# A feed-forward stage of f32 products, rewritten as f16 high and low parts

## The chip, the cores and the metric

The kernel runs on one core of one Trainium2 chip. The metric is the device time of one execution in microseconds. Engines go by the profile's names: PE (TensorE matmul), PEld (its weight loads), DVE (VectorE), ACT (ScalarE), POOL (GpSimd) and SP (SyncE, here the issuer of DMAs).

## The reference, cut to what matters

Two layers work on 8192 tokens (128 sequences of 64) of 128 features: an mLSTM cell with a mixture of experts, then cross attention and a second feed-forward. Only the last step is rewritten. Each of its 8 experts owns 8 fixed positions of every sequence, so 1024 tokens; there is no routing:

```python
# per expert e, on its 1024 tokens; n = layer norm of x
h = silu(n @ w1[e]) * (n @ w3[e])     # 128 -> 352, w1 and w3 f32
x = x + h @ w2[e]                     # 352 -> 128
```

All inputs and the output are f32.

## The kernel before

The kernel runs five stages, each a block of five hand-ordered engine programs that meet through semaphores. An engine runs its own list in order; a wait holds up all that stands behind it on that engine.

- `phase_moe` (first layer's experts): 16 groups with the shared expert, then 39 tiles of 512 sorted tokens. It already works with f16 parts: weights and activations are split into a high and a low f16, and three f16 products (L1119 to L1121, L1132 to L1134) stand for one f32 product. In the tile part DVE makes `hid` (L1302), ACT the high part (L1196), POOL the low part (L1039). SP loads tile j+5 and stores tile j.
- `phase_attention`: 16 groups of 512 tokens, software pipelined. PE order per group is scores, values, the next group's plain products, and so on; ACT exponentiates the scores (`probs`, L1728) and copies values (`v_out`, L1719); DVE takes maxima (`peak_of`, L1791) and divides (`heads_out`, L1815). POOL gathers rows for group g+4 by indirect DMA (L1524). SP stores each finished group in `x3` (L1503) and, at g = 8, loads the f32 weights of the first two experts.
- `phase_ffn`, the last stage: 16 units of 512 tokens (two for each expert). Per unit `turn` (L1991) transposes the normalised tokens, ACT copies them out (L2032), `up` (L1999, L2000) makes three chunks of 128, 128 and 96 hidden features for w1 and w3, ACT applies silu (L2039), DVE multiplies (L2056), `down` (L2008) sums 12 products into `psY`, and DVE adds `x` (L2062). DVE also does the layer norm: statistics (L260, L265) and four subtract-and-scale instructions of 128x128 (L272); POOL only takes the reciprocal root (L284, L286).

PE's order in a unit of the last stage before:

```python
up(p, 0)
up(p, 1)
if p:
    down(p - 1)
if p + 1 < UNITS:
    turn(p + 1)
up(p, 2)
```

All products of this stage are f32; each matmul of the program appears in the trace as two matmul instructions.

Of the kernel before, what the change touches and what calls it, by code (L numbers as in the profile page):

```python
# [910 lines left out]
def phase_moe(nc, sems, a, s, sw, res, front, given, raw, cell):  # L911
# [4 lines left out]
    with ExitStack() as ctx:  # L916
# [522 lines left out]
def phase_attention(nc, sems, a, s, hb, res, ffn, given, raw, sw, cell):  # L1439
# [3 lines left out]
    with ExitStack() as ctx:  # L1443
# [114 lines left out]
        def _(pe):  # L1558
# [129 lines left out]
        def _(act):  # L1688
# [54 lines left out]
            for g in range(LAST):  # L1743
# [21 lines left out]
        def _(v):
# [131 lines left out]
class Ffn:  # L1897

    def __init__(self, nc, ctx, sems, cell, front, raw):
        NC = len(CHUNKS1)  # L1900
        r = self.room = Room(nc, ctx, sems, "ffn")
        self.ident = front.ident
        at = 6 * GROUP
        self.w1 = [*(r.sb(f"w1{w}", [D, FF1]) for w in range(2)), raw[:, at:at + FF1]]
        self.w3 = [*(r.sb(f"w3{w}", [D, FF1]) for w in range(2)), raw[:, at + FF1:at + 2 * FF1]]
        self.w2 = [*(r.sb(f"w2{w}", [P, NC, D]) for w in range(2)),
                   raw[:, at + 2 * FF1:at + 2 * FF1 + NC * D].rearrange("p (c d) -> p c d", c=NC)]
        self.x = [r.sb(f"x{q}", [P, TILES, D]) for q in range(2)]
        self.x += [raw[:, q * GROUP:(q + 1) * GROUP].rearrange("p (t d) -> p t d", t=TILES) for q in range(4, 6)]
        self.xn = cell.xn[1]  # L1910
        self.ln = LayerNorm(r)
        self.w_in, self.x_in = [r.sem(f"w_in{w}") for w in range(3)], [r.sem(f"x_in{q}") for q in range(4)]
        self.xn_done, self.turned, self.xnT_done = r.sem("xn"), r.sem("turned"), r.sem("xnT")
        self.up_done, self.silu_done, self.h_done = r.sem("up"), r.sem("silu"), r.sem("h")
        self.y_done, self.out_done, self.stored = r.sem("y"), r.sem("out"), r.sem2("stored")

    def load(self, sp, s, p):
        for h in range(2):
            sp.dma_start(self.x[p % 4][h * S:(h + 1) * S, :, :], unit_rows(s["x3"], p, h)).then_inc(self.x_in[p % 4], 16)

    def load_weights(self, sp, a, e):
        w = e % 3
        for dst, src in ((self.w1, "f1"), (self.w3, "f3")):
            sp.dma_start(dst[w][:, :], a[src][e]).then_inc(self.w_in[w], 16)
        sp.dma_start(self.w2[w][:, :, :], a["f2"][e]).then_inc(self.w_in[w], 16)
# [278 lines left out]
```

## Time and profile before

| | us |
|---|---|
| timed runs (3) | 1047.19, 1047.42, 1048.82; median 1047.42 |
| profiled execution, span first to last instruction | 1165.9 |
| its own time | recorded as that span alone |
| profiled span less the median | 118.5 |
| last stage in the profile, first transpose to last addition | 1024.69 to 1162.52 = 137.8 |

The profiled execution is 118.5 us longer than the median run. Absolute durations of single instructions are read from it; the share of a whole stage in a timed run is not known.

In the rows, "busy" is the time in which an engine had an instruction under way; PEclk is the granted TensorE clock as a share of 2.4 GHz; "x" counts instructions; a bracket at the end of a row is the engine's idle time before it and the instruction that ended it.

### The profile page before, as it was taken

How to read it: one execution, taken by the hardware profiler on the slowest of the kernel's cores; microseconds unless marked ns; L12 is line 12 of the kernel's file. 1: busy time of each engine (PE TensorE's matmuls, PEld its weight loads, DVE VectorE, ACT ScalarE, POOL GpSimd, SP SyncE). 2: the span in 40 equal slices, each digit the busy share in tenths (PEclk: the TensorE clock that was granted, in tenths of full speed). 3: DMA queues.
4: the chain of work that ended last, by engine and by line, in shares of the span. 5: the costliest groups of instructions: out<-in, count | busy, mean ns of one | idle time of the engine just before them, and what ended most of it. 6: DMA issues, size and time to landing. Idle time of an engine off the chain costs nothing. (4 is left out here: it accounts for less than half of the span.)

```text
span 1165.9 us, 24805 instructions
## 1 busy us (share of the span) xinstructions
PE 969.0 (83%) x9121; PEld 680.7 (58%) x9121; DVE 734.8 (63%) x2271; ACT 535.2 (46%) x848; POOL 505.3 (43%) x566
## 2 busy tenths in 40 slices
PE   6819998667787749999994478888888899989998
PEld 1217776444444426666662267777777778856665
DVE  7676999765566545877774555554555556445553
ACT  2457886432333325666665134453444446332221
POOL 4202675676566652555555773344533531011110
PEclk9869998677879768999998578888888989999999
DMA  8554553321222235333332111101110210024331
GB/s 258 192 148 138 159 165 106 128 89 51 57 61 66 61 89 149 109 124 123 119 119 82 46 33 33 29 28 38 44 31 29 83 49 21 21 65 111 93 93 36
DMA packets 84600, 101.29 MB, mean 87 GB/s; under 512 B 36129, under 2 KB 57313, under 8 KB 83713
## 3 DMA queue, kind: packets, MB, share of 16 engines
q1 hardware_dynamic: 73552, 81.61, 23.5%
q0 software_dynamic: 8192, 16.79, 4.7%
q10 hardware_dynamic: 2736, 1.31, 0.4%
q8 instruction: 73, 1.20, 0.4%
q14 instruction: 47, 0.38, 0.1%
HBM read 64.81 MB, written 30.67 MB: 82 GB/s over the span
## 5 line engine op out<-in xcount | busy, mean ns | idle before, releaser
L1728 ACT ACTIVATE split_table<-attn_psT 128x1024 f32<-128x1024 f32 x64 | 65.5, 1023 | 170.0 <-DMA early_ctxT<-in_ctxT 95.9
L1039 POOL TENSOR_TENSOR moe_h_lo<-moe_hid,moe_h_hi 128x512 f16<-128x512 f32 x78 | 90.3, 1158 | 100.2 <-ACT moe_h_hi L1196 95.4
L1619 PE MATMUL attn_psO<-heads_vheads,split_table 128*64 128x18 f32 x2048 | 87.2, 220 | 30.1 <-issue 30.0
L1302 DVE SCALAR_TENSOR_TENSOR moe_hid<-moe_psU,split_to_hidden,moe_act_g 128x512 f32<-128x512 f32 x110 | 81.0, 748 | 36.5 <-ACT moe_act_g L1190 36.4
L1190 ACT ACTIVATE moe_act_g<-moe_psG,split_unscale 128x512 f32<-128x512 f32 x110 | 75.7, 688 | 59.7 <-PE moe_psU L1121 38.6
L1619 PEld LDWEIGHTS attn_psO<-heads_vheads,split_table 128*64 128x64 f32 x2048 | 78.3, 148 | 41.6 <-issue 39.7
L1791 DVE TENSOR_REDUCE split_table<-attn_psN 128x16 f32<-128x1024 f32 x62 | 75.8, 1222 | 22.4 <-DMA early_ctxT<-in_ctxT 9.6
L1815 DVE RECIPROCAL split_table<-attn_psO 128x16 f32<-128x16 f32 x64 | 16.5, 257 | 112.7 <-PE attn_psO L1619 50.8
L1033 POOL DMA_INDIRECT scratch_xs<-cell_xn,res_row x64 | 63.3, 989 | 42.4 <-DVE res_row L1296 25.2
L1196 ACT ACTIVATE moe_h_hi<-moe_hid 128x512 f16<-128x512 f32 x110 | 68.5, 623 | 24.3 <-DVE moe_hid L1302 23.3
L1033 POOL DMA_INDIRECT scratch_xs<-moe_xn,res_row x64 | 62.6, 978 | 37.2 <-DVE res_row L1296 19.4
L1524 POOL DMA_INDIRECT cell_h<-scratch_ys,res_slot x64 | 62.0, 969 | 19.9 <-issue 19.9
L1524 POOL DMA_INDIRECT cell_y<-scratch_ys,res_slot x64 | 61.8, 966 | 17.7 <-issue 17.4
L284 POOL TENSOR_SCALAR ffn_shifted<-ffn_mv 128x4 f32<-128x4 f32 x16 | 3.6, 228 | 146.7 <-DVE ffn_mv L265 116.5
L1602 PE MATMUL attn_psT<-attn_queries,attn_keys 64*128 64x128 f32 x640 | 64.4, 320 | 1.4 <-issue 1.4
L1602 PEld LDWEIGHTS attn_psT<-attn_queries,attn_keys 64*128 64x128 f32 x640 | 60.2, 213 | 6.9 <-issue 2.0
L284 POOL TENSOR_SCALAR attn_shifted<-attn_mv 128x4 f32<-128x4 f32 x16 | 3.7, 232 | 138.3 <-DVE attn_mv L265 137.5
L1607 PE MATMUL attn_psT<-res_row,attn_sel 64*128 64x128 bf16 x512 | 62.5, 232 | 1.2 <-issue 1.2
L2056 DVE TENSOR_TENSOR ffn_rest_hT<-ffn_rest_act_g,ffn_rest_psU 128x512 f32<-128x512 f32 (+1 forms) x48 | 32.4, 676 | 41.4 <-ACT ffn_rest_act_g L2039 41.4
L1582 PE MATMUL attn_psN<-attn_keys,attn_queries 64*128 64x256 f32 x320 | 53.9, 462 | 4.4 <-DVE split_table L1791 4.4
L1132 PE MATMUL moe_psY<-moe_wt,moe_h_hi 128*128 128x128 f16 x312 | 54.3, 219 | 1.9 <-DVE cell_h L1321 1.9
L2039 ACT ACTIVATE ffn_rest_act_g<-ffn_rest_psG 128x512 f32<-128x512 f32 (+1 forms) x48 | 28.6, 595 | 57.9 <-PE ffn_rest_psU L2000 57.9
(282 smaller groups left out, 2762.9 us busy)
## 6 DMA issues: line engine op xcount, KB each, us to landing
early_ctxT<-in_keys SPq DMA_DIRECT2D x16, 512.0 KB, 3.5
scratch_ys<-cell_h SPq DMA_DIRECT2D x26, 256.0 KB, 2.0
early_ctxT<-in_values SPq DMA_DIRECT2D x8, 544.0 KB, 3.5
mlstm_vals<-in_values SPq DMA_DIRECT2D x8, 544.0 KB, 3.5
res_x<-in_x SPq DMA_DIRECT2D x16, 256.0 KB, 6.2
early_ctxT<-in_ctxT SPq DMA_DIRECT2D x16, 256.0 KB, 6.5
attn_in_ctxT<-attn_in_ctxT SPq DMA_DIRECT2D x64, 64.0 KB
scratch_x<-split_table SPq DMA_DIRECT2D x16, 256.0 KB
```

Source lines behind the costliest of these rows:

```text
L1033: pool.indirect_dma_start(out=s["xs"], out_offset=bass.IndirectOffsetOnAxis(ap=at, axis=0), in_=xn[g % 4][:, t, :], in_offset=None).then_i ...
L1039: pool.tensor_tensor(h_lo[u % 3][c][:, :], hid[u % 2][c][:, :], h_hi[u % 3][c][:, :], ALU.subtract).then_inc(lo_done[c], 1)
L1132: pe.matmul(psY[:, t, :], hi, down_weights(u, 0, c), start=(c == 0), stop=False)
L1190: act.activation(act_g[c][:, :], psG[c][:, :], ACT.Silu, scale=sw.unscale[:, 0:1]).then_inc(silu_done, 1)
L1196: act.activation(h_hi[u % 3][c][:, :], hid[u % 2][c][:, :], ACT.Copy).then_inc(hi_done[c], 1)
L1302: v.scalar_tensor_tensor(out=hid[u % 2][c][:, :], in0=psU[c][:, :], scalar=sw.to_hidden[:, 0:1], in1=act_g[c][:, :], op0=ALU.mult, op1=ALU ...
L1524: pool.indirect_dma_start(out=picks[g % 2][n][:, t, :], out_offset=None, in_=s["ys"], in_offset=bass.IndirectOffsetOnAxis(ap=at, axis=0)). ...
L1602: pe.matmul(psT[:, at:at + P], keys[g % 3][rows, b, 2 * mp:2 * mp + 2, :].rearrange("p m t -> p (m t)"), queries[g % 3][rows, b, :, :].rea ...
L1607: ins = pe.matmul(psT[:, at:at + P], sel[rows, b, mp, :], shift[rows, :], start=False, stop=True)
L1619: ins = pe.matmul(psO[i % 2][b2 * S:(b2 + 1) * S, at * 2 * VW1:(at + 1) * 2 * VW1], probT[i % 2][:, rr, b2, mp, n * S:(n + 1) * S], vheads ...
L1728: act.activation(probT[i % 2][:, :, :, :, :].rearrange("p r b m q -> p (r b m q)"), psT[:, :], ACT.Exp).then_inc(prob_done, 1)
L1791: v.tensor_reduce(peak[:, :, 2 * i:2 * i + 2, :], plain_bank(g, i)[:, :].rearrange("p (r b m t) -> p r b m t", r=HR, b=2, m=HM), AX.X, ALU ...
```

## The change

1. The raw weights `f1`, `f3`, `f2` become one array `f123`, 1088 f32 columns per expert. During the tile part of `phase_moe` SP loads them in 16 pieces (704 or 384 columns) and DVE takes the largest absolute value of each (`largest`). At the head of attention DVE and PE turn these into scale factors (`scale_vector`, `spread_scales`).
2. In attention groups 1 to 10, one expert per group: SP loads an expert's raw weights, ACT writes the high f16 half (`high`), DVE the low half (`low`), SP stores the table of 2176 f16 columns (544 KB) in a scratch `fw` (`keep`).
3. The last stage loads these tables and uses three f16 products for each f32 product; ACT makes the high parts of `x` and `h`, DVE the low part of `x`, POOL the low part of `h`.
4. The layer norm's subtract-and-scale moves from DVE to POOL. PE's order becomes `turn(p+1)`, `up(p)`, `down(p-1)`. There are six token buffers in place of four, and statistics run three units ahead.

```diff
+    def feed(self, sp, a, n, piece):
+        sp.wait_ge(self.piece_read, ONE + n)
+        sp.dma_start(piece[:, 0:last - first], a["f123"][e][:, first:last]).then_inc(self.piece_in, 16)
+    def largest(self, v, n, piece):
+        v.wait_ge(self.piece_in, ONE + 16 * (n + 1))
+        v.tensor_reduce(self.tops[:, n:n + 1], piece[:, 0:last - first], AX.X, ALU.max,
+                        apply_absolute_value=True).then_inc(self.piece_read, 1)
...
+    def load_raw(self, sp, a, e, raw):
+        sp.wait_ge(self.low_done, ONE + e)
+        sp.dma_start(raw[:, :], a["f123"][e]).then_inc(self.raw_in, 16)
+    def high(self, act, e, raw, table):
+        act.wait_ge(self.raw_in, ONE + 16 * (e + 1))
+        act.wait_ge(self.table_out, ONE + 16 * e)
+        for first, last, scale in self.parts():
+            ins = act.activation(table[:, first:last], raw[:, first:last], ACT.Identity, scale=scale)
+        ins.then_inc(self.high_done, 1)
+    def low(self, v, e, raw, table):
+        v.wait_ge(self.high_done, ONE + e + 1)
+        for first, last, scale in self.parts():
+            ins = v.scalar_tensor_tensor(out=table[:, WIDE1 + first:WIDE1 + last], in0=raw[:, first:last], scalar=scale,
+                                         in1=table[:, first:last], op0=ALU.mult, op1=ALU.subtract)
+        ins.then_inc(self.low_done, 1)
+    def keep(self, sp, s, e, table):
+        sp.wait_ge(self.low_done, ONE + e + 1)
+        sp.dma_start(s["fw"][e], table[:, :]).then_inc(self.table_out, 16)
...
@@ phase_moe, SP and DVE
                 store(j)
+                if j % 2 and j // 2 < len(PIECES1):
+                    fw.feed(sp, a, j // 2, piece)
...
+                n = u - GROUPS - 5
+                if n >= 0 and n % 2 == 0 and n // 2 < len(PIECES1):
+                    fw.largest(v, n // 2, piece)
@@ phase_attention, SP, PE, ACT, DVE
+            fw.load_raw(sp, a, 0, ffn.raw)
...
                 store(g)
-                if g == GROUPS // 2:
+                if 1 <= g <= E1:
+                    fw.keep(sp, s, g - 1, ffn.table)
+                if 1 <= g < E1:
+                    fw.load_raw(sp, a, g, ffn.raw)
+                if g == E1 + 1:
+                    sp.wait_ge(fw.table_out, ONE + 16 * E1)
                     for e in range(2):
-                        ffn.load_weights(sp, a, e)
+                        ffn.load_weights(sp, s, e)
...
+            fw.spread_scales(pe, psO[0])
...
                 if two:
                     v_out(g + 2)
+                if 1 <= g <= E1:
+                    fw.high(act, g - 1, ffn.raw, ffn.table)
...
             hb.clear(v, blank)
+            fw.scale_vector(v, psO[0])
             combine(0)
...
                 if now:
                     heads_out(g, 0)
+                if 2 <= g < E1 + 2:
+                    fw.low(v, g - 2, ffn.raw, ffn.table)
@@ phase_ffn, POOL, PE, ACT, DVE
-            for p in range(1, UNITS):
-                ln.root(pool, p, p % 2)
+            def low_part(p, c):
+                pool.wait_ge(hi_done, ONE + NC * p + c + 1)
+                pool.tensor_tensor(h_lo[p % 2][c][0:m, :], hid[c][0:m, :], h_hi[p % 2][c][0:m, :], ALU.subtract).then_inc(lo_done, 1)
+            ln.root(pool, 1, 1)
+            early.normalise(pool, 1)
+            for p in range(UNITS):
+                if p + 2 < UNITS:
+                    ln.root(pool, p + 2, p % 2)
+                    early.normalise(pool, p + 2)
+                if p:
+                    low_part(p - 1, 2)
+                low_part(p, 0)
+                low_part(p, 1)
...
-                pe.matmul(psG[c][0:m, :], w1[w][:, f:f + m], xnT[p % 2][:, :], start=True, stop=True)
-                pe.matmul(psU[c][0:m, :], w3[w][:, f:f + m], xnT[p % 2][:, :], start=True, stop=True).then_inc(up_done, 1)
+                for w, ps in enumerate((psG, psU)):
+                    pe.matmul(ps[c][0:m, :], early.up_weights(e, w, 0, f, m), x_hi[p % 2][:, :], start=True, stop=False)
+                    pe.matmul(ps[c][0:m, :], early.up_weights(e, w, 0, f, m), x_lo[p % 2][:, :], start=False, stop=False)
+                    ins = pe.matmul(ps[c][0:m, :], early.up_weights(e, w, 1, f, m), x_hi[p % 2][:, :], start=False, stop=True)
...
-                pe.wait_ge(h_done, ONE + NC * (p + 1))
+                pe.wait_ge(lo_done, ONE + NC * (p + 1))
...
             for p in range(UNITS):
+                if p + 1 < UNITS:
+                    turn(p + 1)
+                for c in range(NC):
+                    up(p, c)
                 if p:
                     down(p - 1)
...
                 gate(p, 0)
+                if p:
+                    high_part(p - 1, 2)
                 gate(p, 1)
+                high_part(p, 0)
                 gate(p, 2)
+                high_part(p, 1)
...
             for p in range(UNITS):
+                if p + 1 < UNITS:
+                    low_x(p + 1)
+                if p >= 2:
+                    out_(p - 2)
                 gated(p, 0)
-                if p + 1 < UNITS:
-                    early.normalise(v, p + 1)
                 gated(p, 1)
+                if p + 3 < UNITS:
+                    early.statistics(v, p + 3)
                 gated(p, 2)
```

## Rows read from the trace of the kernel before

**Rows 1.** Windows: stretch, length; PE, PEld, DVE, ACT, POOL busy (count), PEclk, DMA share, GB/s.

```profile
455.00:627.00 172.00, 167.65 (x1539) 112.51 (x1537) 136.82 (x197) 115.10 (x193) 90.25 (x78) 1.00 0.36 114
...
690.00:1024.00 334.00, 296.76 (x4223) 253.22 (x4219) 178.91 (x506) 151.63 (x197) 123.43 (x133) 0.88 0.13 37
1024.00:1163.00 139.00, 134.88 (x640) 85.49 (x640) 74.00 (x236) 39.41 (x65) 18.97 (x30) 0.99 0.30 81
```

**Rows 2.** Chain that ended last, within the last stage: start, duration, what.

```profile
1103.45 2.68 PE ffn_rest_psY L2008 x24
...
1111.72 2.68 PE ffn_rest_psY L2008 x24
```

**Rows 3.** Timeline of PE in one expert tile of the first layer.

```profile
574.75 0.38 PE L1119 MATMUL moe_psG<-moe_x_hi,moe_wt 128*128 128x512 f16 x1
...
576.04 0.22 PE L1132 MATMUL moe_psY<-moe_wt,moe_h_hi 128*128 128x128 f16 x1
...
577.38 0.61 PE L1064 MATMUL moe_psT<-split_ident,cell_xn 128*128 128x128 f32 x4
...
577.83 0.38 PE L1119 MATMUL moe_psG<-moe_x_hi,moe_wt 128*128 128x512 f16 x1
```

**Rows 4.** Instruction groups of POOL, by shape: count, busy us, mean ns, idle before.

```profile
L1039 POOL TENSOR_TENSOR moe_h_lo<-moe_hid,moe_h_hi 128x512 f16<-128x512 f32 x78 | 90.3, 1158 | 100.2 <-ACT moe_h_hi L1196 95.4
...
L286 POOL TENSOR_TENSOR ffn_rstd<-ffn_shifted,ffn_power 128x4 f32<-128x4 f32 x16 | 16.6, 1036 | 1.3
...
L284 POOL TENSOR_SCALAR ffn_shifted<-ffn_mv 128x4 f32<-128x4 f32 x16 | 3.6, 228 | 146.7 <-DVE ffn_mv L265 116.5 <-POOLq L1443 30.2
...
L1043 POOL MEMSET cell_h<- 128x512 f32 x1 | 0.5, 524 | 0.0
...
L866 POOL TENSOR_SCALAR cell_next_shifted<-res_mv 128x16 f32<-128x16 f32 x1 | 0.3, 268 | 0.1
```

**Rows 5.** Instruction groups of DVE, by shape.

```profile
L1302 DVE SCALAR_TENSOR_TENSOR moe_hid<-moe_psU,split_to_hidden,moe_act_g 128x512 f32<-128x512 f32 x110 | 81.0, 748 | 36.5 <-ACT moe_act_g L1190 36.4
...
L272 DVE TENSOR_SCALAR cell_xn<-ffn_x,ffn_mv,ffn_rstd 128x128 f32<-128x128 f32 x32 | 8.9, 345 | 6.4 <-POOL ffn_rstd L286 6.4
...
L172 DVE TENSOR_REDUCE split_tops<-split_w_raw 128x1 f32<-128x2304 f32 x3 | 7.4, 2511 | 0.0
```

**Rows 6.** Instruction groups of ACT, by shape.

```profile
L1190 ACT ACTIVATE moe_act_g<-moe_psG,split_unscale 128x512 f32<-128x512 f32 x110 | 75.7, 688 | 59.7 <-PE moe_psU L1121 38.6 <-issue 12.2 <-remote 5.2
L1196 ACT ACTIVATE moe_h_hi<-moe_hid 128x512 f16<-128x512 f32 x110 | 68.5, 623 | 24.3 <-DVE moe_hid L1302 23.3 <-issue 0.9
```

**Rows 7.** Timeline: the last stage's first transposes and products, and its last addition.

```profile
1024.69 0.63 PE L1991 MATMUL ffn_rest_psT<-split_ident,cell_xn 128*128 128x128 f32 x4 [1.71 <-PEq L1443]
1026.10 1.28 PE L1999 MATMUL ffn_rest_psG<-raw_keys,ffn_w 128*128 128x512 f32 x2 [0.78 <-ACT raw_keys L2032]
...
1161.83 0.69 DVE L2062 TENSOR_TENSOR raw_keys<-ffn_rest_psY,raw_keys 128x512 f32<-128x512 f32 x1 [3.04 <-PE ffn_rest_psY L2008]
```

**Rows 8.** Timeline of one attention group: DVE, SP, ACT and PE.

```profile
788.83 0.26 DVE L1815 RECIPROCAL split_table<-attn_psO 128x16 f32<-128x16 f32 x1 [2.08 <-DMA early_ctxT<-in_ctxT]
...
791.06 24.30 SPq L1503 DMA_DIRECT2D scratch_x<-split_table  x2
...
793.69 1.34 ACT L1719 ACTIVATE heads_vheads<-attn_in_ctxT 64x512 f32<-64x512 f32 x2
799.00 1.02 ACT L1728 ACTIVATE split_table<-attn_psT 128x1024 f32<-128x1024 f32 x1 [3.98 <-DMA early_ctxT<-in_ctxT]
...
802.95 0.63 PE L1602 MATMUL attn_psT<-attn_queries,attn_keys 64*128 64x128 f32 x4
```

**Rows 9.** DMA issues: count, KB each, median us from issue to landing.

```profile
scratch_ys<-cell_h SPq DMA_DIRECT2D x26, 256.0 KB, 2.0
early_ctxT<-in_values SPq DMA_DIRECT2D x8, 544.0 KB, 3.5
```

**Rows 10.** Timeline of DVE at the head of attention.

```profile
641.10 1.14 DVE L1770 SCALAR_TENSOR_TENSOR res_x<-cell_h,res_cw,res_x 128x128 f32<-128x128 f32 x4 [6.14 <-DMA cell_h<-scratch_ys,res_slot]
```

More of the change, by code:

```diff
@@ L908, in __init__, with phase_moe @@
         self.mv = ctx.enter_context(nc.sbuf_tensor("res_mv", [P, GROUPS * TILES, 2], F32))
-def phase_moe(nc, sems, a, s, sw, res, front, given, raw, cell):
+def phase_moe(nc, sems, a, s, sw, res, front, given, raw, cell, fw):
     T4 = TILES * E0
@@ L986, in _ @@
             given.room.start_at_one(sp)
+            fw.room.start_at_one(sp)
             given.load(sp)
@@ L1897, with __init__ @@
 class Ffn:
-    def __init__(self, nc, ctx, sems, cell, front, raw):
+    SLOTS = 6
+    def __init__(self, nc, ctx, sems, cell, front, raw, given):
         NC = len(CHUNKS1)
@@ L1902, in __init__ @@
         self.ident = front.ident
+        self.raw, self.table = r.sb("raw", [P, WIDE1]), r.sb("table", [P, 2 * WIDE1], F16)
         at = 6 * GROUP
[L1904 to L1907, printed above, removed]
+        self.tables = [self.raw[:, :].bitcast(F16), self.table[:, :], raw[:, at:at + WIDE1].bitcast(F16)]
@@ L1917, in load, with down_weights @@
+    def down_weights(self, e, part, c, m):
+        at = part * WIDE1 + UP1 + c * D
+        return self.tables[e % 3][0:m, at:at + D]
     def load(self, sp, s, p):
+        q = p % self.SLOTS
         for h in range(2):
[L1919 to L1925, printed above, removed]
@@ L2031, in xnT_out @@
                     act.wait_ge(up_done, ONE + NC * (p - 1))
-                act.activation(xnT[p % 2][:, :], psT[:, :], ACT.Copy).then_inc(xnT_done, 1)
+                act.activation(x_hi[p % 2][:, :], psT[:, :], ACT.Copy, scale=X_SCALE).then_inc(x_hi_done, 1)
             def gate(p, c):
@@ L2038, in gate, with high_part, low_x @@
                     act.wait_ge(h_done, ONE + NC * (p - 1) + c + 1)
[L2039 to L2041 removed]
+                act.activation(act_g[c][0:m, :], psG[c][0:m, :], ACT.Silu, scale=fw.unscale[0:m, 0:1]).then_inc(silu_done, 1)
+            def high_part(p, c):
+                m = CHUNKS1[c][1]
+                act.wait_ge(h_done, ONE + NC * p + c + 1)
+                if p >= 2:
+                    act.wait_ge(y_done, ONE + p - 1)
+                act.activation(h_hi[p % 2][c][0:m, :], hid[c][0:m, :], ACT.Copy).then_inc(hi_done, 1)
+            xT_out(0)
             for p in range(UNITS):
+                if p + 1 < UNITS:
+                    xT_out(p + 1)
                 gate(p, 0)
+                if p:
+                    high_part(p - 1, 2)
                 gate(p, 1)
[L2045 to L2046 removed]
+                high_part(p, 0)
                 gate(p, 2)
+                high_part(p, 1)
+            high_part(UNITS - 1, 2)
         @block.vector
         def _(v):
+            def low_x(p):
+                v.wait_ge(x_hi_done, ONE + p + 1)
+                v.scalar_tensor_tensor(out=x_lo[p % 2][:, :], in0=psT[:, :], scalar=X_SCALE, in1=x_hi[p % 2][:, :],
+                                       op0=ALU.mult, op1=ALU.subtract).then_inc(x_lo_done, 1)
             def gated(p, c):
```

166 lines of the change are left out of this document (115 added, 51 removed).

## The prediction

> **What bounds the kernel now.** I read the busy time by stage first. In the last stage PE is busy 134.88 of 139 us at a granted clock of 0.99, POOL only 18.97; in the expert tiles, which already use f16 parts, PE is full too, at 1.00; in attention PE is busy 296.76 of 334 us at 0.88 [rows 1]. The chain that ended last shows PE alone in the last stage: two successive `down` begin 8.26 us apart, as they do all along the stage, and PE has no gap in that time [rows 2]. So a unit costs 8.27 us of PE, and 16 units with head and tail run from the first transpose to the last addition, 1024.69 to 1162.52, 137.8 us [rows 7]. Nothing in it runs below full clock but the head. The span of the profiled execution, 1165.9 us, is 118.5 us above the median of the runs; I take the difference that I forecast as the same number of microseconds in both, because the stage that changes most is at full clock and without stalls in the profile, so it has little room to be shorter in a run.
>
> **PE's part of the change.** An expert tile shows what f16 thirds cost. Six `up` matmuls of 512 columns start at 574.75 and the next kind starts at 576.04: 1.29 us, 0.215 each. The 24 `down` matmuls of 128 columns take 576.04 to 577.38, 0.056 each. Four transposes take 577.38 to 577.83, 0.45 us [rows 3]. The new unit has 3 chunks x 2 weights x 3 = 18 `up`, 4 x 3 x 3 = 36 `down` and the same transposes: 18 x 0.215 + 36 x 0.056 + 0.45 = 6.3 us. If PE stayed the bound, a unit would fall from 8.27 to 6.3, and 16 units by 31 us. That is the best end.
>
> **POOL's part.** This is the term that I think decides. POOL now runs, per unit, one small add (0.228), the root (1.036), four subtract-and-scale instructions of 128x128 and three low parts of 1.158 [rows 4]; for the 96-row chunk I take the full price, as 512 columns are walked all the same. Without the four: 0.23 + 1.04 + 3.47 = 4.74 us, and about 0.08 us between instructions (the idle in front of the 16 roots is 1.3 us in all [rows 4]), eight times, 0.6. The trace has no tensor-scalar of 128 columns on POOL. Bounds: a memset of 512 columns takes 0.524, about 1 ns a column at most, so 0.228 + 124 x 0.85 = 0.33 is the low end (0.85 ns: 0.524 less a 0.1 start); the small tensor-scalar grows from 0.228 at 4 columns to 0.268 at 16, 3.3 ns a column, so 0.60 to 0.64 is the high end; two sources cost 1.158 for 512 columns, 2.3 ns [rows 4]. With one source, between memset and two sources, I take 1.5 ns: 0.41 us, nearest to the low end because the 12 columns behind the high end are short and strided. Four make 1.64. POOL's unit: 4.74 + 0.6 + 1.64 = 7.0 us, more than PE's 6.3. In its list POOL must finish root, normalise and the third low part of unit p-1 before it can begin the first low part of unit p, and PE's `down` waits for that third low part; with POOL never idle, PE waits about 0.7 us a unit. DVE (five passes of 0.75, 3.75 us [rows 5], and the statistics that it already makes) and ACT (three silu of 0.688, three high parts of 0.623 and one copy out of PSUM, priced as a silu, 4.6 us [rows 6]) stay under 6.3.
>
> I chained the four engines' lists with these prices from the first transpose. `up` of unit 0 can now begin only when POOL has normalised unit 1, since `turn(1)` stands ahead of it: about 3.9 instead of 1.4 us after the first transpose [rows 7]; the first `down` ends at 17.9 instead of 15.2. Then twelve units at 7.0, the last three (no more norms) at 6.6, 6.2 and 3.9, and the addition: 17.9 + 84 + 16.7 + 0.8 = 119.4 against 137.8, **18.4 us less**. For unit 0 the clock may still be at half, as the first product's 1.28 us shows [rows 7]; I give back 1.0.
>
> **What the edits ahead of the stage cost.** In the expert tiles, 16 pieces: DVE's maximum of 704 columns is at most 2.511 x 704 / 2304 = 0.77 us [rows 5], every second tile. DVE is busy 136.82 of 172 us [rows 1], PE needs the low x it makes one tile later, and the pieces are asked for two tiles ahead. SP's wait for the piece just read delays a tile load by about 1.6 us, against loads five tiles ahead. I price it at nothing; without that cover it is 8 x (0.77 + 0.42) = 9.5 us. At the head of attention DVE stands idle 6.14 us for the first gather [rows 10]; the new chain is eight small operations and two round trips to PE and hides there unless they average over 0.6 us each.
>
> In attention each of 8 groups gets, on ACT, two passes over 1088 columns, 0.623 x 1088 / 512 = 1.32 us [rows 6], and on DVE 0.748 x 1088 / 512 = 1.59 us [rows 5]. DVE's sits ahead of an idle of 2.08 us [rows 8], so it hides. ACT's follows `v_out`, which ends at 795.03; the next exponential starts at 799.00 after 3.98 us idle [rows 8]. But ACT also waits for the raw weights, whose load SP issues behind the group's store at 791.06 and the 544 KB table store. A 256 KB transfer lands in 2.0 us and one of 544 KB in 3.5 [rows 9]: all three together between 3.5 (side by side) and 9.0 (one after another), by the slope of the two rows 7.7. Then ACT runs its 1.32 us from 798.8, and the exponential comes at 800.1, 1.1 us late; PE wants it at 802.95 [rows 8], when it would have been done at 801.1. So it hides too, barely. I charge 0.2 us to each of 8 groups, 1.5 us; the bounds are 0 and 8 x (1.32 + 1.59) = 23 us.
>
> **Sum:** -18.4 + 1.0 + 1.5 = -16 us: 1150 in the profile, 1047.4 - 16 = **1031 us**.
>
> **Rivals.** (a) **POOL is as quick as DVE at one source.** The same instruction takes 0.345 us on DVE [rows 5]. Then POOL needs 6.7 a unit, the two engines alternate, and the stage ends at 116 instead of 119.4: 1028 us. The Trainium skill, GPSIMD Engine Reference, section Engine selection, says just this, one-input work on GpSimd at roughly line rate; no row here shows it. For it: memset's slope. Against: two operations with two pointers per instruction. (b) **POOL is slow at it**, 0.6 us, the slope of the small form. A unit is 7.75 us, the stage 130: 1042 us. (c) **Slower: the splitting lands on attention's path.** Place: ACT's wait for the raw weights, ahead of the next group's first exponential. The 3.98 us idle there may exist only in the profiled execution, which is 118.5 us longer; in a run with tighter groups the load comes late and PE waits for both passes. It decides from 2.2 us a group (17.5 / 8); at its full 23 us the result is 1031 + 21 = 1052 us. For it: the load stands behind two stores. Against: PE itself shows 37 us less than full in that stage, and DVE and ACT are under 55% there [rows 1]. (d) **Almost no change:** waits of about 0.7 us a unit let the clock fall and give back what POOL leaves, so the stage runs at about 8.2 us a unit: 1046 us. Against: the clock stays at 0.99 to 1.00 where PE is at 97% [rows 1]; I expect 90%.
>
> **Chances.** Forecast 0.50, (a) 0.22, (b) 0.12, (c) 0.10, (d) 0.06. The range: low end (a) without the costs ahead of the stage and with the lowest POOL price, 1023; high end (b) with 3 us more in attention, 1045. A change under 0.2%, 2 us, can't be told from none (the three runs spread over 1.6 us). Faster: forecast, (a), (b), and a little of (c), 0.86; the same: (d), 0.05; slower: 0.09. PE at two thirds of its f32 cost is seen in the trace; what is not seen is POOL's price, and that moves the time by 10 us, seldom its sign.
>
> **What would show it.** Right: `down` 7.0 us apart in the last stage, POOL busy over 90% there with the normalise at 0.41 us, PE waiting before `down` for the low part. Wrong: PE without gaps (a), normalise at 0.6 (b), ACT's `high` idle on a DMA and longer groups in attention (c), a clock under 0.9 in the last stage (d). Groups 1 to 10 of attention as long as the later ones would prove the splitting hidden.

## The result, and the profile after

The change made the kernel slower: 1065.86 us (median of 4 runs, 1063.45 to 1074.26) against 1047.31 (4 runs, 1046.39 to 1048.82), a ratio of 1.0182 [1.0142, 1.0222]. The profiled execution of after spans 1061.6 us.

The profile of before that the prediction was read from was an odd execution, 118.5 us longer than the timed runs. So before was profiled again (run b0_again: 1049.57 us, span 1047.8), and the differences below are against that second profile.

> The kernel before, once more, for a second profile. If the profiled execution of 1165.9 us was an odd one, this one spans about 1047 us, attention groups far from its head are about 16.8 us long with PE busy throughout (as the groups without splitting are in the changed kernel), and a unit of the last stage is 8.27 us. If the profile itself slows this kernel, it spans about 1166 us again.

The excess of the first profile lies where the prediction read its idle times. Its attention, from its first instruction to the first transpose of the last stage, takes 395.6 us against 321.5 in b0_again, 74 of the 118.5 us; 44 lie ahead of attention and none in the last stage (137.8 against 138.2). One attention group, from `v_out` to `v_out`, in the first profile and in the second (columns as in [rows 1]):

```profile
769.83:793.69 23.86, 20.70 (x277) 17.61 (x277) 12.69 (x36) 10.65 (x16) 10.40 (x12) 0.86 0.12 34
...
754.53:771.34 16.81, 16.81 (x283) 14.50 (x279) 12.88 (x36) 10.66 (x15) 10.36 (x12) 1.00 0.19 49
```

In an ordinary execution PE is busy in the whole group, so whatever holds PE up there costs time.

Windows of that second profile of before, attention and last stage (columns as in [rows 1]):

```profile
584.68:906.18 321.50, 284.85 (x4402) 241.79 (x4403) 214.56 (x612) 172.37 (x225) 166.76 (x181) 0.92 0.17 47
906.18:1044.40 138.22, 134.88 (x640) 85.43 (x640) 73.99 (x236) 39.45 (x65) 18.93 (x30) 0.99 0.31 82
```

The same windows of after:

```profile
582.62:921.78 339.16, 292.58 (x4409) 244.83 (x4409) 234.42 (x637) 180.56 (x241) 167.51 (x181) 0.91 0.24 71
921.78:1058.15 136.37, 109.79 (x928) 71.87 (x928) 73.82 (x192) 68.62 (x113) 119.88 (x138) 0.95 0.32 83
```

Attention starts 2.06 us earlier and lasts 17.7 us longer; the last stage, which was to give 18.4 us, gives 1.8. Together -2.1 + 17.7 - 1.8 = 13.8 us, the difference of the two spans.

**The last stage.** PE's busy time fell from 134.88 to 109.79 us, POOL's rose from 18.93 to 119.88. POOL's groups there in after, by shape (columns as in [rows 4]; the first three answer to rows of that group):

```profile
L2107 POOL TENSOR_TENSOR ffn_rest_h_lo<-ffn_rest_hid,ffn_rest_h_hi 128x512 f16<-128x512 f32 x32 | 36.6, 1159 | 0.9
...
L369 POOL TENSOR_TENSOR ffn_rstd<-ffn_shifted,ffn_power 128x4 f32<-128x4 f32 x15 | 15.6, 1042 | 1.2
...
L367 POOL TENSOR_SCALAR ffn_shifted<-ffn_mv 128x4 f32<-128x4 f32 x15 | 3.5, 232 | 32.1 <-POOLq L1533 30.4 <-DVE ffn_mv L348 1.7
...
L355 POOL TENSOR_SCALAR cell_xn<-ffn_x,ffn_mv,ffn_rstd 128x128 f32<-128x128 f32 x20 | 15.7, 800 | 0.9 <-POOL ffn_rstd L369 0.9
```

The old items have the old prices. The new one, subtract-and-scale, takes 0.80 us. POOL's timeline shows a whole unit with no gap over 0.2 us:

```profile
952.78 0.23 POOL L367 TENSOR_SCALAR ffn_shifted<-ffn_mv 128x4 f32<-128x4 f32 x1
953.10 1.04 POOL L369 TENSOR_TENSOR ffn_rstd<-ffn_shifted,ffn_power 128x4 f32<-128x4 f32 x1
954.32 3.14 POOL L355 TENSOR_SCALAR cell_xn<-attn_in_ctxT,ffn_mv,ffn_rstd 128x128 f32<-128x128 f32 x4 [0.18 <-POOL ffn_rstd L369]
957.43 3.38 POOL L2107 TENSOR_TENSOR ffn_rest_h_lo<-ffn_rest_hid,ffn_rest_h_hi 96x512 f16<-96x512 f32 x3
960.79 0.23 POOL L367 TENSOR_SCALAR ffn_shifted<-ffn_mv 128x4 f32<-128x4 f32 x1
```

From 952.78 to 960.79 is 8.01 us, a unit; [rows 2] had 8.26. The granted clock is 1.00 in these units (950 to 960, and again 1010 to 1041). The 0.95 of the whole stage comes from its head: 0.51 in the first 8.2 us, and 0.50 to 0.51 from 941 to 947, behind a wait of PE for POOL's low part ahead of the first `down`:

```profile
940.96 0.29 PE L2149 MATMUL ffn_rest_psY<-ffn_raw,ffn_rest_h_hi 128*128 128x128 f16 x1 [3.53 <-POOL ffn_rest_h_lo L2107]
...
940.94:945.00 4.06, 4.04 (x38) 4.05 (x39) 0.75 (x1) 0.00 (x0) 3.44 (x4) 0.50 0.00 0
```

This first `down` takes 4.0 us and ends 23.2 us after the stage's first transpose; the later ones take 2.2.

**Attention.** What the engines waited for in after (total, times, longest), from 640 to 930:

```profile
ACT ffn_table L289 <- DMA ffn_raw<-in_f: 22.3, 7, 4.0
```

L289 is the pass that writes the high half; it runs in groups 1 to 8, the low half's in groups 2 to 9. The timeline of ACT and SP in three groups of after:

```profile
681.97 1.33 ACT L1816 ACTIVATE heads_vheads<-attn_in_ctxT 64x512 f32<-64x512 f32 x2
687.29 1.39 ACT L289 ACTIVATE ffn_table<-ffn_raw,ffnw_all 128x704 f16<-128x704 f32 x2 [3.98 <-DMA ffn_raw<-in_f]
688.58 1.00 ACT L1825 ACTIVATE split_table<-attn_psT 128x1024 f32<-128x1024 f32 x1
...
702.14 0.37 SPq L1594 DMA_DIRECT2D scratch_x<-split_table  x1
702.55 0.59 SPq L301 DMA_DIRECT2D scratch_fw<-ffn_table  x1
703.18 0.45 SPq L283 DMA_DIRECT2D ffn_raw<-in_f  x1
...
708.57 1.39 ACT L289 ACTIVATE ffn_table<-ffn_raw,ffnw_all 128x704 f16<-128x704 f32 x2 [2.55 <-DMA ffn_raw<-in_f]
```

SP issues the raw load (L283) only behind the group's store (L1594) and the store of the last table (L301), and ACT stands 2.55 us for it. While it stands, the exponential behind it (L1825) stands too. In the second profile of before, ACT's timeline has this at the same place:

```profile
754.53 1.34 ACT L1719 ACTIVATE heads_vheads<-attn_in_ctxT 64x512 f32<-64x512 f32 x2
757.16 1.03 ACT L1728 ACTIVATE split_table<-attn_psT 128x1024 f32<-128x1024 f32 x1 [1.28 <-PE attn_psT L1607]
```

So the idle time that was to hide all this is 1.28 us, not the 3.98 of [rows 8]. Windows of after: the last group without a split, and the first three with one:

```profile
660.77:677.58 16.81, 16.81 (x277) 14.50 (x276) 13.85 (x36) 11.81 (x17) 9.59 (x11) 1.00 0.18 49
677.58:700.29 22.71, 20.30 (x277) 16.56 (x276) 16.14 (x41) 11.92 (x17) 12.02 (x13) 0.85 0.28 85
700.29:718.42 18.13, 17.08 (x277) 14.46 (x276) 13.32 (x36) 11.60 (x17) 8.85 (x11) 1.00 0.35 107
718.42:740.99 22.57, 20.36 (x277) 16.67 (x276) 16.14 (x41) 11.81 (x17) 12.14 (x13) 0.85 0.28 87
```

A wait of 2.55 us makes 16.81 into 18.13. The groups with waits of 3.98 and 3.79 us take 22.71 and 22.57: there the granted clock is 0.85. Two shorter windows inside the last of them: first PE stands still for 2.21 of 5 us, then the clock is at the lower of its two levels:

```profile
727.00:732.00 5.00, 2.79 (x37) 2.26 (x37) 4.30 (x12) 4.07 (x6) 2.77 (x3) 0.99 0.20 59
732.00:737.00 5.00, 5.00 (x40) 3.38 (x42) 2.08 (x6) 3.50 (x6) 0.00 (x0) 0.50 0.00 0
```

The eight groups with a split, by the starts of DVE's last addition (678.71 to 833.88), take 155.2 us, 20.7 over eight of 16.81. In the other six the clock is 1.00 and they take 17.4 to 19.2 us. (The head of attention, from its first instruction to the first of these additions, is 3.2 us shorter in this profile than in b0_again; it is 82.0 us in e5 and 79.5 in e2, so it differs between executions.)

### The profile page after: what moved, and what is told of

It is laid out like the page before. It is cut to its first block and busy times, and to the rows that moved or that the text cites. A ratio compares the mean times of both kernels' runs of the same rounds, so it can differ in the third digit from the quotient of the medians.

```text
span 1061.6 us, 25704 instructions
## 1 busy us (share of the span) xinstructions
PE 881.4 (83%) x9415; PEld 626.8 (59%) x9415; DVE 766.2 (72%) x2268; ACT 572.0 (54%) x912; POOL 608.0 (57%) x674
## 5 line engine op out<-in xcount | busy, mean ns | idle before, releaser
L1825 ACT ACTIVATE split_table<-attn_psT 128x1024 f32<-128x1024 f32 x64 | 65.3, 1020 | 92.1 <-PE attn_psT L1703 86.3
L1620 POOL DMA_INDIRECT cell_h<-scratch_ys,res_slot x64 | 62.5, 976 | 19.2 <-issue 19.2
L1715 PE MATMUL attn_psO<-heads_vheads,split_table 128*64 128x18 f32 x2048 | 72.9, 214 | 0.1
L1620 POOL DMA_INDIRECT cell_y<-scratch_ys,res_slot x64 | 62.6, 979 | 17.7 <-issue 17.4
L1715 PEld LDWEIGHTS attn_psO<-heads_vheads,split_table 128*64 128x64 f32 x2048 | 66.5, 140 | 9.0 <-issue 7.8
L1698 PE MATMUL attn_psT<-attn_queries,attn_keys 64*128 64x128 f32 x640 | 56.2, 294 | 4.8 <-ACT split_table L1825 4.8
L2107 POOL TENSOR_TENSOR ffn_rest_h_lo<-ffn_rest_hid,ffn_rest_h_hi 128x512 f16<-128x512 f32 (+1 forms) x48 | 54.5, 1158 | 6.2 <-ACT ffn_rest_h_hi L2187 5.3
L1698 PEld LDWEIGHTS attn_psT<-attn_queries,attn_keys 64*128 64x128 f32 x640 | 52.8, 188 | 8.8 <-issue 6.3
L1219 PE MATMUL moe_psY<-moe_wt,moe_h_hi 128*128 128x128 f16 x312 | 54.3, 219 | 1.9 <-DVE cell_h L1408 1.9
L800 ACT ACTIVATE mlstm_decay<-mlstm_psA 128x512 f32<-128x512 f32 x64 | 37.8, 591 | 32.9 <-PE mlstm_psA L750 32.9
L1220 PE MATMUL moe_psY<-moe_wt,moe_h_hi 128*128 128x128 f16 x312 | 54.3, 219 | 0.0
L1221 PE MATMUL moe_psY<-moe_wt,moe_h_lo 128*128 128x128 f16 x312 | 54.3, 219 | 0.0
L1678 PE MATMUL attn_psN<-attn_keys,attn_queries 64*128 64x256 f32 x320 | 48.1, 421 | 5.5 <-DVE split_table L1892 5.4
L826 DVE SCALAR_TENSOR_TENSOR mlstm_cT<-mlstm_psS,mlstm_decay 128x512 f32<-128x512 f32 x64 | 43.4, 677 | 11.7 <-PE mlstm_psS L755 11.1
```

The costliest lines, as they stand in the source:

```text
L1620: pool.indirect_dma_start(out=picks[g % 2][n][:, t, :], out_offset=None, in_=s["ys"], in_offset=bass.IndirectOffsetOnAxis(ap=at, axis=0)). ...
L1678: ins = pe.matmul(bank[:, rr * 512 + b2 * HM * S:rr * 512 + (b2 + 1) * HM * S], queries[g % 3][rows, b, :, :].rearrange("p n t -> p (n t)" ...
L1698: pe.matmul(psT[:, at:at + P], keys[g % 3][rows, b, 2 * mp:2 * mp + 2, :].rearrange("p m t -> p (m t)"), queries[g % 3][rows, b, :, :].rea ...
L1715: ins = pe.matmul(psO[i % 2][b2 * S:(b2 + 1) * S, at * 2 * VW1:(at + 1) * 2 * VW1], probT[i % 2][:, rr, b2, mp, n * S:(n + 1) * S], vheads ...
L1825: act.activation(probT[i % 2][:, :, :, :, :].rearrange("p r b m q -> p (r b m q)"), psT[:, :], ACT.Exp).then_inc(prob_done, 1)
L2107: pool.tensor_tensor(h_lo[p % 2][c][0:m, :], hid[c][0:m, :], h_hi[p % 2][c][0:m, :], ALU.subtract).then_inc(lo_done, 1)
```

## The experiments

Two theories stood. **P:** POOL's price of subtract-and-scale sets the last stage. **A:** the late raw load sets the attention groups. Rivals: in the last stage PE or the lower clock, in attention the work of the two splitting passes itself.

**e1, subtract-and-scale back on DVE.**

```diff
-            early.normalise(pool, 1)
...
-                    early.normalise(pool, p + 2)
...
+            early.normalise(v, 1)
...
                 gated(p, 0)
+                if p + 2 < UNITS:
+                    early.normalise(v, p + 2)
                 gated(p, 1)
```

> The changed kernel with subtract-and-scale of the last stage back on DVE (between the first two chunks of a unit); POOL keeps the root and the low parts. Theory: POOL's four instructions of 0.80 us hold the last stage at 8.0 us a unit; without them POOL needs about 5 us and a unit falls to 6.5 to 6.7, the stage from about 136 to 112 to 115, the time by 20 to 24 us, to about 1043. Rival: the low parts' chain through ACT and POOL or the single token buffer holds the unit; then it stays at 8.0 and the time at 1066.

Measured: 1042.06 us, ratio 0.994 [0.9923, 0.9958], 24 us under after; units of 6.70 us, the last stage 115.3 instead of 136.4. P holds. But PE's own 6.3 us was not reached. The chain that ended last runs through DVE alone:

```profile
953.27 2.31 DVE cell_xn L355 x4
...
959.98 2.31 DVE cell_xn L355 x4
```

Four that took 0.345 each [rows 5] take 2.31 together. The instructions of this line, ns min/median/max:

```profile
L355 DVE TENSOR_SCALAR cell_xn<-raw_keys,ffn_mv,ffn_rstd x24: 333/340/2217, 926.4 to 1015.6; 128x128 f32<-128x128 f32 x24
```

The median is the old price; single instructions take up to 2.2 us, this longest one beside two of POOL's low parts in a row. e9 and e10 take this up.

**e2, the table's store and the raw load ahead of the group's store.**

```diff
             for g in range(GROUPS):
-                store(g)
                 if 1 <= g <= E1:
                     fw.keep(sp, s, g - 1, ffn.table)
                 if 1 <= g < E1:
                     fw.load_raw(sp, a, g, ffn.raw)
+                store(g)
```

> The changed kernel with SP issuing the table store and the next raw load ahead of the group's own store, which it waits for 4 us later. Theory: ACT stands idle for the raw weights (22 us in 7 waits) because the load is issued late; issued about 4 us earlier it has landed when ACT comes, groups 2 to 9 fall from 18 to 22.7 us to about 17 to 17.5, and the time falls by 14 to 19 us, to about 1049. Rival A: ACT's and DVE's own passes (1.4 and 1.5 us a group) are the cost: groups stay at 18 or more and the time falls by less than 6 us. Rival B: the extra transfers slow the gathers: the same.

Measured: 1049.89 us (6 runs), ratio 1.0023 [1.0002, 1.0045], 16 us under after. Units stay at 8.0. The timeline of SP and ACT shows the load now 3.6 us ahead of the store, and ACT's pass straight behind the copy of values:

```profile
711.09 0.43 SPq L283 DMA_DIRECT2D ffn_raw<-in_f  x1
714.70 0.37 SPq L1594 DMA_DIRECT2D scratch_x<-split_table  x1
...
717.24 1.33 ACT L1816 ACTIVATE heads_vheads<-attn_in_ctxT 64x512 f32<-64x512 f32 x2
718.60 1.39 ACT L289 ACTIVATE ffn_table<-ffn_raw,ffnw_all 128x704 f16<-128x704 f32 x2
```

Groups take 17.43 us: A holds, for 15.8 of the 20.7 us. (ACT's pass also waits for the table's store, which e2 moves too; the profile puts the wait down to the raw load.) The other 0.62 a group is at DVE and POOL:

```profile
718.04 2.68 DVE L355 TENSOR_SCALAR cell_xn<-res_x,attn_mv,attn_rstd 128x128 f32<-128x128 f32 x4
...
718.58 1.28 POOL L1625 TENSOR_TENSOR res_x<-res_x,attn_in_bp 128x512 f32<-128x512 f32 x1
```

DVE's low pass stands ahead of the statistics, POOL's list starts later by about that pass, and its 1.28 us addition falls on DVE's four instructions, which take 1.30 us in b0_again; e7 tests this.

**e3, one expert's split only**; every unit reads the table of expert 0.

```diff
-                if 1 <= g <= E1:
-                    fw.keep(sp, s, g - 1, ffn.table)
-                if 1 <= g < E1:
-                    fw.load_raw(sp, a, g, ffn.raw)
+                if g == 1:
+                    fw.keep(sp, s, 0, ffn.table)
...
-                    fw.high(act, g - 1, ffn.raw, ffn.table)
+                if g == 1:
...
+                    fw.high(act, 0, ffn.raw, ffn.table)
...
-                if 2 <= g < E1 + 2:
-                    fw.low(v, g - 2, ffn.raw, ffn.table)
+                if g == 2:
+                    fw.low(v, 0, ffn.raw, ffn.table)
...
-        sp.dma_start(self.tables[e % 3], s["fw"][e])
+        sp.dma_start(self.tables[e % 3], s["fw"][0])
```

> The changed kernel with only expert 0 split; seven of the eight splits, their raw loads and table stores are left out, and all units of the last stage load expert 0's table. It prices all of the splitting in attention. Theory: seven eighths of about 21 us, so about 1047 us, with groups of 16.8 us from the third on; and 2 to 4 us below the reordered kernel, which keeps the passes. Rival: the attention stage is longer for another reason (scales, the room taken); then it stays near 1066.

Measured: 1047.37 us (10 runs), ratio 0.9986 [0.997, 1.0003]; groups take 16.81 from the third on, units 8.0. What attention lost is lost by the splits and not by the changed code around them; alone, this does not tell the load from the passes; e2 and e7 do.

**e5, e1 and e2 together.**

> Both mends in one kernel: the subtract-and-scale back on DVE and SP's table store and raw load ahead of the group's store. Theory: the two costs are separate (one in attention, one in the last stage) and add up: 16 us and 24 us off the changed kernel, 1066 - 40 = about 1026 us, 0.98 of the kernel before, attention groups 17.4 us and units 6.7 us. Rival: they share something (the room on DVE, the transfers); then it stays at 1032 or more.

Measured: 1031.52 us, ratio 0.9804 [0.978, 0.9827]; groups 17.43, units 6.70, so each part gives in its stage what it gave alone. The total is 5 us above 1065.9 - 16 - 24 = 1026, at the edge of the rival's 1032. In the profile these 5 us lie outside both parts: attention starts 2.5 us later than in e1 and e2 (585.4 against 582.9), and its head is 2.6 us longer, as it differs between executions.

**e6, POOL's price by form.** Units take turns: the old form, two constants, one operation with a pointer, one with a constant, and one instruction of 512 columns; four in five units are not normalised.

```diff
+        if form == 1:
+            for t in range(TILES):
+                ins = eng.tensor_scalar(xn[:, t, :], x[:, t, :], 0.5, 0.125, ALU.subtract, ALU.mult)
+        if form == 2:
+            for t in range(TILES):
+                ins = eng.tensor_scalar(xn[:, t, :], x[:, t, :], self.ln.rstd[p % 2][:, t:t + 1], None, ALU.mult)
+        if form == 3:
+            for t in range(TILES):
+                ins = eng.tensor_scalar(xn[:, t, :], x[:, t, :], 0.125, None, ALU.mult)
+        if form == 4:
+            ins = eng.tensor_scalar(xn[:, :, :], x[:, :, :], 0.5, 0.125, ALU.subtract, ALU.mult)
```

> The changed kernel with four of five units' subtract-and-scale on POOL in another form, so leaving out the proper norm there: two constants in place of two per-token pointers; one pointer and one operation; one constant and one operation; one instruction of 512 columns with two constants. It measures POOL's price. Theory A: the two pointers make it slow: with constants 0.33 to 0.45 us, one pointer about 0.5 to 0.6. Theory B: POOL pays per column whatever the form: 0.75 to 0.80 us in each 128-column form, and 512 columns about 0.23 + 508 x 4.6 ns = 2.5 us.

Measured: 1059.07 us (one run). POOL's groups by shape, in that order:

```profile
L355 POOL TENSOR_SCALAR cell_xn<-attn_in_ctxT,ffn_mv,ffn_rstd 128x128 f32<-128x128 f32 x8 | 6.3, 797 | 0.4 <-POOL ffn_rstd L369 0.4
L2058 POOL TENSOR_SCALAR cell_xn<-ffn_x 128x128 f32<-128x128 f32 x8 | 5.0, 648 | 0.7 <-PE ffn_rest_psT L2144 0.5 <-POOL ffn_rstd L369 0.2
L2061 POOL TENSOR_SCALAR cell_xn<-ffn_x,ffn_rstd 128x128 f32<-128x128 f32 x8 | 4.7, 607 | 0.4 <-POOL ffn_rstd L369 0.4
L2064 POOL TENSOR_SCALAR cell_xn<-raw_keys 128x128 f32<-128x128 f32 x8 | 4.1, 533 | 0.3 <-POOL ffn_rstd L369 0.3
L2066 POOL TENSOR_SCALAR cell_xn<-raw_keys 128x512 f32<-128x512 f32 x2 | 3.9, 1940 | 0.3 <-POOL ffn_rstd L369 0.3
```

A second operation costs 0.115 us (648 less 533), a pointer 0.075 (607 less 533, and half of 797 less 648). With two constants 384 more columns cost 1.29 us, 3.4 ns each. The small instruction of [rows 4] is one operation with one constant, the cheapest of these forms: from its 0.228 us at 4 columns to 0.533 at 128 it grows by 2.5 ns a column, less than the 3.3 that it shows from 4 to 16. Neither theory holds: the forms differ, so it is not a price by column alone, and even with constants none is below 0.53.

**e7, e5 with DVE's low pass behind the statistics.**

```diff
-                if 2 <= g < E1 + 2:
-                    fw.low(v, g - 2, ffn.raw, ffn.table)
                 if three:
                     statistics(g + 3)
+                if 2 <= g < E1 + 2:
+                    fw.low(v, g - 2, ffn.raw, ffn.table)
```

> Both mends, and DVE's low pass of the weights put behind the group's statistics in place of ahead of them. The reordered kernel's groups are still 17.43 us against 16.81: its trace shows DVE's subtract-and-scale in attention at 2.68 us for four in place of 1.30, under POOL's bias add, which the later statistics have moved onto it. Theory: with the statistics at their old place POOL's list keeps its time, the two don't meet, and groups fall to 16.8 to 17.0 us; time 3 to 5 us under the kernel with both mends alone, about 1022. Rival: the two passes' own time is the cost; then groups stay at 17.4.

Measured: 1027.8 us, ratio 0.9784 [0.9768, 0.98]. The window of the eight groups has PE without a gap at full clock, 16.81 each:

```profile
684.30:818.79 134.49, 134.49 (x2202) 116.00 (x2203) 115.90 (x304) 93.34 (x126) 89.32 (x90) 1.00 0.35 108
```

So the splitting hides completely once two lists have another order; the last 0.62 us a group came from the place of DVE's pass. The time is 3.7 us under e5, as expected; the 1022 came from e5's expected 1026.

**e8, e7 with ACT's third high part ahead of the next unit's first silu.**

```diff
-                gate(p, 0)
                 if p:
                     high_part(p - 1, 2)
+                gate(p, 0)
                 gate(p, 1)
```

> The last one, and on ACT the high part of a unit's third chunk ahead of the next unit's first silu in place of behind it. Theory: a unit of 6.7 us still waits in front of its last products for the low part of the third chunk, which follows that high part; earlier it leaves PE's own 6.3 us plus what DVE loses under POOL: 6.3 to 6.5 a unit, 3 to 6 us less in all. Rival: DVE is the bound by now (0.60 us for each subtract-and-scale beside POOL, about 7 us of 6.7 a unit busy); then a unit stays at 6.7.

Measured: 1026.61 us (1022.73 to 1026.95), ratio 0.9758 [0.9733, 0.9782]; units of 6.81 us instead of 6.70. No gain that can be told from e7: the high part was not what held the unit up.

**e9, e7 with POOL's low part of h cut to 4 columns**; PE reads the high part in its place.

```diff
-                pool.tensor_tensor(h_lo[p % 2][c][0:m, :], hid[c][0:m, :], h_hi[p % 2][c][0:m, :], ALU.subtract).then_inc(lo_done, 1)
+                pool.tensor_tensor(h_lo[p % 2][c][0:m, 0:4], hid[c][0:m, 0:4], h_hi[p % 2][c][0:m, 0:4], ALU.subtract).then_inc(lo_done, 1)
...
-                        hi, lo = h_hi[p % 2][c][0:m, cols], h_lo[p % 2][c][0:m, cols]
+                        hi, lo = h_hi[p % 2][c][0:m, cols], h_hi[p % 2][c][0:m, cols]
```

> Against e7_low_late, POOL's low part of h in the last stage is cut from 512 columns to 4, and PE reads the high part in its place: the low part's product is left out, PE does the same number of matmuls. Theory A: in e1, e5 and e7 one of the four subtract-and-scale instructions of DVE stands still until POOL's 1.16 us low part is through (2.31 us for four, where three take 0.34), and that makes DVE the bound of a unit. Then the four take 1.36 us, DVE falls to about 5.4 us a unit, PE's own 6.3 us is left as the bound, and the time falls by 16 x 0.4 = 6 us to about 1022. Theory B: DVE's instructions are long for another reason (PE or ACT reading the same memory): four still take 2.3 us, units stay at 6.70 and the time at about 1028.

Measured: 1017.37 us, 10 us under e7. DVE's line again, min/median/max:

```profile
L355 DVE TENSOR_SCALAR cell_xn<-raw_keys,ffn_mv,ffn_rstd x24: 335/341/344, 912.8 to 994.7; 128x128 f32<-128x128 f32 x24
```

The longest is now 344 ns. PE's timeline has its transposes, one set a unit, 6.35 us apart, and a window of 70 us shows PE without a gap:

```profile
920.79 0.61 PE L2125 MATMUL ffn_rest_psT<-split_ident,cell_xn 128*128 128x128 f32 x4
927.14 0.60 PE L2125 MATMUL ffn_rest_psT<-split_ident,cell_xn 128*128 128x128 f32 x4
```

```profile
930.00:1000.00 70.00, 70.00 (x640) 48.14 (x639) 60.41 (x180) 46.73 (x78) 19.22 (x53) 1.00 0.45 116
```

So PE's own unit is 6.35 us, and theory A of this run holds. Of the 8.3 us between the two profiled spans 6.4 lie in the last stage (115.24 against 108.85 us), near the 6 expected; the rest lies ahead of it, where nothing was edited. e9 also takes work off POOL, for whose low parts PE waits. But in e7 POOL had room and DVE had none, in nine units (columns as in [rows 1]):

```profile
928.10:988.43 60.33, 58.46 (x523) 38.53 (x522) 59.41 (x154) 37.86 (x63) 42.05 (x46) 1.00 0.44 117
```

In one of them POOL and DVE stand like this:

```profile
954.38 1.15 POOL L2107 TENSOR_TENSOR ffn_rest_h_lo<-ffn_rest_hid,ffn_rest_h_hi 96x512 f16<-96x512 f32 x1
955.74 1.16 POOL L2107 TENSOR_TENSOR ffn_rest_h_lo<-ffn_rest_hid,ffn_rest_h_hi 128x512 f16<-128x512 f32 x1 [0.21 <-ACT ffn_rest_h_hi L2185]
...
954.92 2.31 DVE L355 TENSOR_SCALAR cell_xn<-raw_keys,ffn_mv,ffn_rstd 128x128 f32<-128x128 f32 x4
```

DVE's four begin inside the first low part and end 0.33 us behind the second. By themselves they take 0.70, 0.34, 1.18 and 0.33 us: two of them are long (not one, as was expected), and each of the two ends 0.08 us behind the end of a low part. That fits an instruction that stands still until POOL's is through.

**e10, DVE's subtract-and-scale with two source tensors** (the scale as a broadcast source).

```diff
-            ins = v.tensor_scalar(y[:, t, :], x[:, t, :], self.mv[k][:, t, 0:1], self.rstd[k][:, t:t + 1],
-                                  ALU.subtract, ALU.mult)
+            ins = v.scalar_tensor_tensor(out=y[:, t, :], in0=x[:, t, :], scalar=self.mv[k][:, t, 0:1],
+                                         in1=self.rstd[k][:, t:t + 1].to_broadcast([P, P]), op0=ALU.subtract, op1=ALU.mult)
```

> Against e7_low_late, DVE's subtract-and-scale is written with two source tensors (the scale as a broadcast second source), in attention and in the last stage. Theory A: only the one-source form stands behind POOL; the two-source multiply of the last stage (0.739 us in e1, 0.748 in the first profile) never grew beside POOL. By its size (0.74 us for 512 columns, about 1 ns a column over 0.25) one of 128 columns takes about 0.37 us, four 1.5 instead of 2.31: units 6.3 to 6.4, about 1022 us; attention groups at 16.81. Theory B: any DVE instruction at that place stands behind POOL: units stay at 6.70, about 1028 us. A broadcast source that is read more slowly would make it longer than 1030.

Measured: 1027.03 us, ratio 0.9789 [0.9764, 0.9814], as e7; units of 6.84, and four still take about 2.45 us:

```profile
L355 DVE SCALAR_TENSOR_TENSOR cell_xn<-raw_keys,ffn_mv,ffn_rstd x24: 338/346/2290, 914.8 to 1004.9; 128x128 f32<-128x128 f32 x24
```

Theory A of this run falls: the number of sources isn't what counts. The multiply that never grows (L2212, 0.751 us at most here) takes one source from PSUM; this one takes both from SBUF. The Trainium skill, SBUF — State Buffer, section Who interferes with whom, says that DVE shares one pair of SBUF ports with GpSimd, that whoever issues first holds it for a whole instruction, and that a DVE instruction contends when both its inputs lie in SBUF and GpSimd's instruction reads SBUF, or in its two-port modes, which `tensor_scalar` can enter. e1, e7, e9 and e10 agree with that; in which mode the one-source form ran, no run shows.

**e11, subtract-and-scale on ACT**, with POOL making the offset.

```diff
+                pool.tensor_scalar(minus[k][:, :], ln.mv[k][:, :, 0], -1.0, None, ALU.mult).then_inc(minus_done, 1)
...
+                pool.tensor_tensor(offs[k][:, :], minus[k][:, :], ln.rstd[k][:, :], ALU.mult).then_inc(off_done, 1)
...
+                    ins = act.activation(xn[:, t, :], x[n % early.SLOTS][:, t, :], ACT.Identity,
+                                         bias=offs[k][:, t:t + 1], scale=ln.rstd[k][:, t:t + 1])
```

> Against e7_low_late, the last stage's subtract-and-scale goes to ACT (scale and offset in one activation of 128 columns, four a unit, ahead of the second silu); POOL makes the offset with two small operations, about 0.5 us a unit. DVE loses 2.3 us a unit. Theory A: ACT has room (4.6 us of 6.7 busy, plus 4 x about 0.3 = 1.2), so PE's 6.3 us becomes the bound: about 1022 us. Theory B: ACT's list is part of the chain from product to silu to high part to low part, and 1.2 us ahead of the second silu delays PE's next product: units 6.7 or longer, 1028 us or more.

Measured: 1034.53 us, ratio 0.9845 [0.9814, 0.9875]; units of 7.30. Its row, and ACT's waits from 915 to 1010:

```profile
L2205 ACT ACTIVATE cell_xn<-raw_keys,ffn_rest_offs,ffn_rstd 128x128 f32<-128x128 f32 x24 | 9.9, 482 | 6.3 <-POOL ffn_rest_offs L2118 6.3
...
ACT cell_xn L2205 <- POOL ffn_rest_offs L2118: 13.4, 13, 1.7
```

The instruction takes 0.48 us, not 0.3, and now ACT waits for POOL's offset, about 1 us a unit, with its silu behind it: theory B.

The best versions are e7, e8 and e10, about 1027 us, 2% under before. Bringing DVE's four into a gap of POOL's list was not tried; by e9's 6.35 against 6.70 it could be worth 16 x 0.35 = 5.6 us.

## Why the prediction was wrong

- **"Four make 1.64" (POOL's part).** This step failed. I took 0.41 us an instruction and bounded it at 0.64; it is 0.80. e6 takes it apart: one operation with one constant costs 0.533, a second operation 0.115 more, two pointers 0.149, together 0.797. I had named the operations and pointers against rival (a) and priced them at nothing, and both ends of my bounds came from cheaper forms (the low end also leans on a start of 0.1 us that no row shows). A unit is 8.01 instead of 7.0, and the twelve units in the middle of the stage take 96.2 us instead of 84. Rival (b) had the mechanism and too low a price. Of rival (a) the Trainium skill, GPSIMD Engine Reference, section Engine selection, says the same; here GpSimd needs 0.80 us where DVE needs 0.345, so page and measurement differ.
- **"The first `down` ends at 17.9"** failed with it: it ends at 23.2. POOL's list in front of it is longer by its price, PE stands 3.53 us, and then the granted clock is 0.50 through that `down`; the 1.0 us that I gave back was for the first products alone. With the last three units and the addition at 17.0 (priced at 17.5) the stage is 23.2 + 96.2 + 17.0 = 136.4 instead of 119.4, and gave 1.8 us instead of 18.4.
- **"So it hides too, barely" (attention).** This step failed too, as rival (c) said, and at about its price: 20.7 us in the eight groups, priced at 23 less what was already charged. The landing that I estimated, 7.7 us behind SP's store at 791.06, was fair: in after ACT goes on 6.4 us (702.14 to 708.57) to 7.9 us behind SP's store. What failed is the cover: 3.98 us of idle read from one group of an execution that was 118.5 us too long. In an ordinary one it is 1.28. DVE's cover of 2.08 us is likewise 0.60 there, and PE, whose room I put against rival (c), has none. I saw the excess and took differences as safe for the last stage, then used the same profile's idle time in attention, where 74 us of the excess lay.
- **The bound of 23 us for attention** held and its reason did not: it was to be two passes with no cover, and the passes cost nothing in e7's order. The wait costs most of it, and twice: once itself, once more by the granted clock, in the two groups where ACT waits nearly 4 us and the clock is 0.85.
- **PE's 6.3 us a unit** was right: 6.35 in e9. (That is 0.76 of 8.27, three quarters; the prediction's last words on chances call it two thirds.) **The maxima and the head of attention at nothing** were right as far as the profiles tell: attention starts at 582.6 to 585.9 us in all versions with the maxima, at 584.7 without, and its head is no longer than before's.
- **Rival (d)** happened in the head of the stage only: there the granted clock fell to 0.50 behind a wait. In the units behind it PE waits more than I had, the clock is 1.00, and POOL sets the unit.
- **DVE "stays under 6.3"** holds for its own durations; with POOL's three low parts beside it (e1, e7) it is the bound at 6.70. Nothing in the prediction allowed for that; it did not matter in after, where the four instructions are on POOL.

The sum by its own steps, with what the runs showed: -1.8 for -18.4 + 1.0, +17.7 for +1.5, -2.1 for 0: +13.8 us in the profiles. The -2.1, and -3.2 in the +17.7, differ between executions. The medians differ by 18.6; the profiled execution of after was the fastest of its four, 2.4 us under its median, and b0_again 2.3 us above before's. Neither failed step alone makes the change slower by much: with attention mended it is even with before (e2), with POOL's part mended a little faster (e1).

## What to carry to other kernels

An idle time that is to hide new work must be read from an execution whose span agrees with the timed runs; where it doesn't, take the cover as nothing and price the change again. Before elementwise work goes to GpSimd, price it by its form (operations, pointers, columns), and look for the DVE instructions that will run beside it. A load for which a full stage must wait goes ahead of stores in its queue: this order alone was worth 16 us here.

## What was not expected of the hardware

- GpSimd's tensor-scalar on 128x128 f32 takes 0.53 to 0.80 us by its form and 1.94 for 512 columns with two constants.
- A DVE instruction of 0.34 us that runs into GpSimd's 1.16 us subtraction takes 0.70 or 1.18 us and ends just behind it; beside two in a row it takes up to 2.2. It takes 0.34 again when that subtraction is cut to 4 columns.
- A wait of ACT of 2.55 us, with 1.05 us of idle PE in its group, left the granted clock at 1.00 (18.13 us), and so did one of 3.6 us with 2.1 of idle PE (19.21); waits of 3.8 and 4.0 us, with PE idle for 2.2 and 2.4, came with a clock of 0.85 (22.6 and 22.7). The lower clock cost more than the longer wait itself.
